# Cross-attention and routed experts: scores of batch 1 in their own banks, and the mask loaded for VectorE from batch 3 on

## The reference

```python
# x (16, 100, 128), ctx (16, 1444, 128), mask (16, 1444) with 1 at keys left out
def xattn(input, memory, mask, w_input, dot_scale):
    input_dot = einsum('bqd,od->bqo', input, w_input)
    cross_dot = einsum('bqd,bkd->bqk', input * dot_scale, memory)
    att = input_dot + cross_dot - 1e+30 * mask[:, None, :]
    return einsum('bqk,bkd->bqd', softmax(att), memory)

def ffn(x):                         # 8 experts of width 512, the best 2 of each row
    gates, indices = top_k(softmax(einsum('bsd,ed->bse', x, W_router)), 2)
    gates = gates / sum(gates)
    return sum over the experts e of weight_e * (silu(x Wg_e) * (x Wu_e)) Wd_e

x = x + tanh(g_xattn) * xattn(layernorm(x), ctx, mask, w_input, dot_scale)
x = x + tanh(g_ffn) * ffn(layernorm(x))
```

## Time and profile before

| | |
|---|---|
| median of three runs | 260.19 us (258.18 to 261.61) |
| the profiled execution | 261.3 us, its span 259.5 us |
| TensorE busy | 231.3 us, 89% of the span |
| VectorE, ScalarE, GpSimd busy | 138.6, 115.1 and 114.0 us |
| chain that ended last | PE 73%, DMA 6%, issue 6%, DVE 6%, POOL 4% |
| attention steps | to about 136 us of the span |
| experts | to about 242 us |
| gather and add | the rest |

### The profile page before, as it was taken

How to read it: one execution, slowest core, us unless ns; L and a number is a source line. 1 busy time by engine, 2 the same in 40 slices (tenths; PEclk the granted TensorE clock), 3 DMA queues, 4 the chain that set the end, 5 groups by cost and what they waited for, 6 DMA issues and landing times.

```text
span 259.5 us, 5485 instructions
## 1 busy us (share of the span) xinstructions
PE 231.3 (89%) x1448; PEld 181.9 (70%) x1449; DVE 138.6 (53%) x499; ACT 115.1 (44%) x269; POOL 114.0 (44%) x197
## 2 busy tenths in 40 slices
PE   7979999999999999979998899799999999999200
PEld 6437877677777677847868688688888789888100
DVE  4237565766868768685686567333433333432043
ACT  3024553446554445623646435355554455545000
POOL 4451433365675566544456764443352333224300
PEclk9979999999999999997999999999999999999755
DMA  6997677788786776835923521232111111000194
GB/s 171 330 380 222 191 258 207 244 282 246 235 320 201 260 268 198 305 114 145 377 71 86 196 77 34 63 82 63 45 51 53 41 43 39 30 23 21 37 240 132
DMA packets 19107, 41.39 MB, mean 159 GB/s; under 512 B 3574, under 2 KB 10018, under 8 KB 19070
## 3 DMA queue, kind: packets, MB, share of 16 engines
q1 hardware_dynamic: 15796, 36.37, 44.0%
q0 software_dynamic: 2560, 3.77, 4.6%
q10 hardware_dynamic: 726, 0.94, 1.4%
HBM read 34.82 MB, written 6.24 MB: 158 GB/s over the span
## 4 chain that ended last, share of the span: by engine, by line
PE 73%; DMA 6%; issue 6%; DVE 6%; POOL 4%; ACT 1%; SPq 1%; ACTq 1%; DVEq 0%; POOLq 0%
PE psum L1084 16%; PE psum L1064 12%; PE psum L1178 10%; PE psum L1156 6%; PE psum L1158 5%; PE psum L1157 5%; PE psum L1073 5%; PE psum L1167 4%; PE psum L1052 4%; DMA ctx_sb<-results 3%; PE psum L1146 1%; POOL slots L553 1%; DMA w_lo<-in_mask 1%; PE psum L1092 1%; DMA slots<-pair_rows,slot_i 1%
## 5 line engine op out<-in xcount | busy, mean ns | idle before, releaser
L1084 PE MATMUL psum<-ctx_sb,probsT 128*100 128x128 f32 (+1 forms) x384 | 53.9, 286 | 0.0
L610 POOL DMA_INDIRECT results<-y_sb,dest x32 | 30.7, 959 | 52.4 <-DVE dest L968 24.9
L1084 PEld LDWEIGHTS psum<-ctx_sb,probsT 128*100 128x100 f32 (+1 forms) x384 | 45.0, 170 | 3.4 <-issue 0.7
L979 DVE SCALAR_TENSOR_TENSOR scores<-probs,row_in,psum 128x512 f32<-128x512 f32 x32 | 23.9, 747 | 38.4 <-ACT probs L696 38.2
L1064 PE MATMUL psum<-ctxT,qT 128*100 128x512 f32 (+1 forms) x96 | 44.1, 597 | 0.0
L635 ACT ACTIVATE probsT<-psum 128x400 f32<-128x400 f32 x48 | 20.7, 504 | 52.2 <-PE psum L1073 52.1
L553 POOL DMA_INDIRECT slots<-pair_rows,slot_i x32 | 33.9, 1061 | 18.6 <-DMA slots<-pair_rows,slot_i 9.4
L786 DVE CUSTOM_DVE_ANT_0 scores<-psum,zeros 100x1444 f32<-100x1444 f32 x16 | 26.6, 1661 | 18.7 <-PE psum L1064 18.7
L1178 PE MATMUL psum<-w_down,hidT 128*128 x256 | 34.3, 277 | 1.9 <-issue 0.7
L696 ACT ACTIVATE probs<-psum 128x512 f32<-128x512 f32 x32 | 19.2, 599 | 35.3 <-PE psum L1158 35.3
L1178 PEld LDWEIGHTS psum<-w_down,hidT 128*128 128x128 f32 x256 | 31.1, 192 | 2.6 <-issue 2.6
(11 more groups left out here) (134 smaller groups left out, 306.6 us busy)
## 6 DMA issues: line engine op xcount, KB each, us to landing
ctxT<-in_ctx_cols SPq DMA_DIRECT2D x16, 722.0 KB, 4.7
ctx_sb<-in_ctx SPq DMA_DIRECT2D x16, 704.0 KB
w_raw<-in_w_experts SPq DMA_DIRECT2D x16, 256.0 KB, 3.4
row_in<-slots SPq DMA_DIRECT2D x32, 65.0 KB, 1.9
w_down<-in_w_experts SPq DMA_DIRECT2D x4, 512.0 KB, 7.2
slots<-empty SPq DMA_DIRECT2D x8, 195.0 KB, 2.2
ctx_sb<-results SPq DMA_DIRECT2D x4, 192.0 KB, 5.1
ctx_sb<-results ACTq DMA_DIRECT2D x4, 192.0 KB, 5.9
```

Of the source, the lines that this page charges most:

```text
L610: nc.gpsimd.indirect_dma_start(results, bass.IndirectOffsetOnAxis(ap=dest[:, s:s + 1], axis=0), y_sb[:, s, :], None).then_inc(y_stored[s], 16)
L979: nc.vector.scalar_tensor_tensor(out=hidden[k % 2], in0=silu[k % 2], scalar=row_in[:, o, D:D + 1], in1=up_ps[k % 2], op0=ALU.mult, op1=ALU ...
L1084: last = nc.tensor.matmul(attn_ps[0:Q, 0:D], probsT[0:rows[c], c, :], ctx_sb[0:rows[c], b % CTX_RING, c, :], start=(c == 0), stop=(c == CH ...
```

## The change

Six things change.

1. The scores of batch 1 go to banks 3 to 5 (`second_scores_ps`), so they no longer wait for VectorE's reduce of batch 0. These are the banks of the transposes; the first transposes of probabilities wait for `scores_done` of batch 1, with eight matmuls of no use ahead of them, and scores of batch 1 wait until ScalarE has copied q out of bank 3.
2. For batch 0 the scores come first and the mask is added behind them. Its columns are loaded ahead of the mask.
3. The mask is added by TensorE for batches 0 to 2 alone (`PE_MASKS` = 3). ScalarE scales the mask by -1e30 once more into a tile, stores it to a tensor in memory (`mask_scaled`), and from batch 3 on SP loads one row of it into 100 partitions of `maskb` (two transfers, 96 and 4 partitions, three batches ahead). VectorE's reduce adds `maskb` where it added `zeros`, and waits for its load.
4. The tables are spread: `tile_counts` stays in step 12, `tile_runs` goes to step 13, `tile_rows` stays in 14, `tile_experts` goes to 15, and the gates go ahead of the tables of their step.
5. In step 15 GpSimd makes the rows of batch 13 first and scatters those of batch 10 then.
6. In the experts, the transpose of tile 8's rows comes behind down of tile 5 on TensorE and ScalarE alike, the expert's number is read earlier for three tiles, and down of tile 30 writes to a bank of its own (`other_y_ps`), so that down of tile 31 need not wait for its copy.

The order on VectorE in step 12 and at the head of step 13, before: the last of `top_two`, `tile_counts` and `tile_runs`, then the gates, then the residual (L763).

```diff
--- before.py
+++ after.py
@@ -28,6 +28,8 @@
+MASK_RING = 3
+PE_MASKS = 3
...
@@ -115,10 +119,12 @@
+        other_y_ps = psum[:, 6, 0:D]
...
-        zeros = sb("zeros", [Q, K])
+        maskb = sb("maskb", [Q, MASK_RING, K])
+        zeros = maskb[:, (PE_MASKS + MASK_RING - 1) % MASK_RING, :]
...
@@ -336,6 +346,14 @@
+        def scores_home(b):
+            return second_scores_ps if b == 1 else scores_ps
+        def y_home(k):
+            return other_y_ps if k == T - 2 else y_ps
         def pairs(j, m):
...
@@ -366,6 +384,11 @@
+            def load_mask(b):
+                s = b % MASK_RING
+                sp.dma_start(maskb[0:MAIN, s, :], mask_scaled[b, 0:K].partition_broadcast(MAIN)).then_inc(mask_in[s], 16)
+                sp.dma_start(maskb[MAIN:Q, s, :], mask_scaled[b, 0:K].partition_broadcast(Q - MAIN)).then_inc(mask_in[s], 16)
             def load_weights(b):
...
@@ -376,10 +399,10 @@
             load_x(0)
+            load_cols(0)
             sp.dma_start(mask_raw[0:B * PIECES, :], pieces).then_inc(mask_loaded, 16)
...
             sp.dma_start(mask_raw[LOW:mask_rows, :], pieces).then_inc(mask_loaded, 16)
-            load_cols(0)
...
@@ -390,12 +413,16 @@
             load_x(3)
+            sp.wait_ge(scaled_stored, 16)
+            load_mask(PE_MASKS)
...
                 sp.wait_ge(scores_done, b + 1)
+                if b + MASK_RING < B:
+                    load_mask(b + MASK_RING)
                 for c in ROUNDED.get(b + 1, ()):
...
@@ -570,13 +597,12 @@
             for b in range(B):
-                if b == B - 1:
-                    pair_landed(0)
-                    scatter(b - 5)
                 if b >= 2:
...
                     normalise2(b - 2)
-                if 5 <= b < B - 1:
+                if b == B - 1:
+                    pair_landed(0)
+                if 5 <= b:
                     scatter(b - 5)
...
@@ -675,6 +701,9 @@
             copy_qT(0)
+            nc.scalar.activation(mask_f32, mask_raw[0:B * PIECES, :], ACT.Copy, scale=NEG).then_inc(scaled_done, 1)
+            act.wait_ge(scaled_done, 1)
+            act.dma_start(mask_scaled.rearrange("b (t n) -> (b t) n", n=PIECE), mask_f32).then_inc(scaled_stored, 16)
             for b in range(B):
...
@@ -700,14 +729,14 @@
                     nc.scalar.activation(hidT[:, (k - 1) % 2, :], hidT_ps, ACT.Copy).then_inc(hidT_done, 1)
-                if k == EARLY - 1:
-                    rowT_high(i, k + 1)
                 if k - 2 >= 0:
...
                     wait(act, y_stored[s], i * 16 + 16 * ((k - 2) // YRING))
-                    nc.scalar.activation(y_sb[:, s, :], y_ps, ACT.Copy).then_inc(y_done, 1)
+                    nc.scalar.activation(y_sb[:, s, :], y_home(k - 2), ACT.Copy).then_inc(y_done, 1)
+                if k == EARLY - 1:
+                    rowT_high(i, k + 1)
...
@@ -783,7 +812,10 @@
                 apart(dve)
-                nc.vector.tensor_tensor_reduce(out=scores[0:Q, :], in0=scores_ps[0:Q, 0:K], in1=zeros[:, :],
+                if b >= PE_MASKS:
+                    dve.wait_ge(mask_in[b % MASK_RING], 32 * ((b - PE_MASKS) // MASK_RING + 1))
+                addend = maskb[:, b % MASK_RING, :] if b >= PE_MASKS else zeros
+                nc.vector.tensor_tensor_reduce(out=scores[0:Q, :], in0=scores_home(b)[0:Q, 0:K], in1=addend,
                                                scale=1.0, scalar=LOWEST, op0=ALU.add, op1=ALU.max,
...
@@ -1032,40 +1066,54 @@
-            def keep_warm(n):
+            def keep_warm(n, into=ring_ps[GROUPS - 1][:, (GROUP - 1) * Q:GROUP * Q]):
                 for _ in range(n):
-                    nc.tensor.matmul(ring_ps[GROUPS - 1][:, (GROUP - 1) * Q:GROUP * Q], identity[:, :], identity[:, 0:Q], start=True, stop=True)
+                    nc.tensor.matmul(into, identity[:, :], identity[:, 0:Q], start=True, stop=True)
...
-            def add_mask(b):
+            def add_mask(b, start):
                 pe.wait_ge(select_done, 1)
                 pe.wait_ge(mask_lo_done, 1)
-                wait(pe, scores_done, b)
-                wait(pe, rank_done, (b - 3) // 2)
                 for t, n in enumerate(range(0, K, PIECE)):
                     m = min(PIECE, K - n)
-                    nc.tensor.matmul(scores_ps[0:Q, n:n + m], select[:, b * PIECES + t:b * PIECES + t + 1].to_broadcast([mask_rows, Q]), mask_split[:, 0:m], start=True, stop=False)
-            def score(b):
-                if b > 0:
-                    add_mask(b)
+                    last = nc.tensor.matmul(scores_home(b)[0:Q, n:n + m],
+                                            select[:, b * PIECES + t:b * PIECES + t + 1].to_broadcast([mask_rows, Q]),
+                                            mask_split[:, 0:m], start=start, stop=not start)
+                return last
+            def add_scores(b, start, stop):
                 pe.wait_ge(qT_done, b + 1)
                 pe.wait_ge(col_loaded[b % COL_RING], 16 * (b // COL_RING + 1))
-                wait(pe, scores_done, b)
-                wait(pe, rank_done, (b - 3) // 2)
                 for n in range(0, K, 512):
                     m = min(512, K - n)
-                    last = nc.tensor.matmul(scores_ps[0:Q, n:n + m], qT[:, b % 2, :], ctxT[:, b % COL_RING, n:n + m],
-                                            start=False, stop=True)
-                last.then_inc(scores_raw, 1)
+                    last = nc.tensor.matmul(scores_home(b)[0:Q, n:n + m], qT[:, b % 2, :], ctxT[:, b % COL_RING, n:n + m],
+                                            start=start, stop=stop)
+                return last
+            def score(b):
+                if b == 0:
+                    add_scores(0, True, False)
+                    add_mask(0, False).then_inc(scores_raw, 1)
+                    return
+                if b == 1:
+                    pe.wait_ge(qT_done, 2)
+                else:
+                    pe.wait_ge(scores_done, b)
+                    wait(pe, rank_done, (b - 3) // 2)
+                if b < PE_MASKS:
+                    add_mask(b, True)
+                add_scores(b, b >= PE_MASKS, True).then_inc(scores_raw, 1)
             def transpose_probs(b):
+                if b == 0:
+                    keep_warm(8, attn_ps[:, 0:Q])
+                    pe.wait_ge(scores_done, 2)
                 pe.wait_ge(probs_done, b + 1)
...
@@ -1130,10 +1178,9 @@
-            keep_warm(10)
-            add_mask(0)
+            keep_warm(11)
             transpose_q(0)
-            keep_warm(2)
+            keep_warm(1)
             for b in range(B):
...
@@ -1167,15 +1218,20 @@
-            def down(i, k):
+            def down(i, k, e=None):
                 n = i * YRING + k
                 o = k % 2
-                e = pe.value_load(tile_expert[0:1, bass.ds(n, 1)], min_val=0, max_val=E - 1)
+                e = expert_of(i, k) if e is None else e
                 pe.wait_ge(hidT_done, n + 1)
-                wait(pe, y_done, n)
+                if k == T - 2:
+                    pe.wait_ge(rank_done, LAST + 1)
+                elif k == T - 1:
+                    pe.wait_ge(y_done, T - 2)
+                else:
+                    wait(pe, y_done, n)
                 for c in range(FC):
-                    last = nc.tensor.matmul(y_ps, hidT[:, o, c * P:(c + 1) * P], w_down[:, bass.ds(e * F + c * P, P)],
+                    last = nc.tensor.matmul(y_home(k), hidT[:, o, c * P:(c + 1) * P], w_down[:, bass.ds(e * F + c * P, P)],
                                             start=(c == 0), stop=(c == FC - 1))
...
@@ -1204,16 +1259,19 @@
                 if k - 2 >= 0:
-                    down(i, k - 2)
+                    down(i, k - 2, e)
+                if k == EARLY - 1:
+                    transpose_rows(i, k + 1)
...
             transpose_xn2(B - 3)
+            pe.wait_ge(experts_ready, 1)
+            first = expert_of(0, 0)
             transpose_probs(B - 1)
             route(B - 3)
-            pe.wait_ge(experts_ready, 1)
             pe.wait_ge(w_lo_done, B)
-            gate_up(0, 0)
+            gate_up(0, 0, first)
             ranks(LAST - 1)
...
```

More of the change, by code:

```diff
@@ L94, in build @@
     slots = nc.dram_tensor("slots", [DUMMY + P, ROW], F32).ap()
+    mask_scaled = nc.dram_tensor("mask_scaled", [B, mask.shape[1]], F32).ap()
     results = nc.dram_tensor("results", [2 * TOKENS + YRING * P, D], F32).ap()
@@ L234, in build @@
         mask_lo_done = sem("mask_lo_done")
+        scaled_done = sem("scaled_done")
+        scaled_stored = sem("scaled_stored")
+        mask_in = [sem(f"mask_in{s}") for s in range(MASK_RING)]
         ctx_loaded = [sem(f"ctx_loaded{s}") for s in range(CTX_RING)]
@@ L928, in step @@
                     tile_rows(False)
+                if b == 15:
                     tile_experts(False)
[L930 to L931 removed]
                 for c in split[1:]:
                     split_weights(c)
[L935 removed]
+            nc.vector.memset(zeros, 0.0)
             dve.wait_ge(identity_done, 1)
```

21 lines of the change are left out of this document (12 added, 9 removed).

## The result

The changed kernel took 277.02 us (median of four runs, 276.31 to 278.06), the kernel before 259.68 beside it. The ratio is 1.067 (95% interval 1.059 to 1.075): slower, 23 us above the forecast. The profiled execution took 276.75 us, its span 275.0.

The account below looks back on a forecast made before the run. TensorE's own order was taken to bound the kernel (73% of the span). 0.4 + 1.6 + 1.6 + 2.97 - 1.06 + 0.1 + 0.4 + 0.4 + 0.2 = 6.6 us off 260.2 gave 253.6 us, range 249.5 to 259.5.

Parts of the forecast that it names:

- The prediction's rival: Attention's DMA queue becomes the bound because of the mask loads: 257.6 us (chance 10%) or 265.7 us (chance 8%).
- 10 us as slack: DMA queue in attention: loads ordered two to three steps early were counted as 10 us it could owe without loss.
- the bad case: DMA queue in attention: each mask load takes 3.8 us, giving 265.7 us in all, chance 8%.
- The start: Batches 0 and 1: scores 0 start at 8.0 us (7.7 to 9.0), gaining 0.4 us.
- Masks on TensorE: Steps 3 to 15 without mask matmuls: gain 1.6 us in 3 and 4, 1.6 in even 6 to 12, odd 0.
- the chain from the residual: Attention steps: VectorE's residual through GpSimd's pair_rows to TensorE's transpose of xn2 takes 3.33 us, so odd steps gain 0.
- Tables: Table operations moved out of step 12: step 13 gains 2.97 us, 1.50 of it the clock; step 14 loses 1.06.
- the 1.50 that I had charged for this: Step 14: TensorE idles 1.89 us, so its clock falls there and costs 1.50 us.
- Step 15: Rows made ahead of scatters on GpSimd: gain 0.1 us, with the last exp as the next limit.
- Experts: Expert tiles: gains of 0.4 us at tile 8, 0.4 at the last down, 0.2 from expert numbers loaded earlier.
- the longer wait that the prediction had named for late scatters: Tile 8 of the experts: would wait longer if GpSimd's queue came late; costed at nothing.
- The two terms of the last tiles: End of the experts: 0.4 us from the last down not awaiting ScalarE's copy, 0.2 from expert numbers loaded earlier.

## Why the prediction was wrong

**DMA: the step that failed.** The prediction's rival had the right mechanism: the queue becomes the bound, and it "would show on ScalarE first, waiting for w_raw". Its price was wrong, in the sentence "at the 363 GB/s that a full stretch showed (share 1.01) 1.6 us. Then 5.94 + 1.6 = 7.54, as long as the new step". It took the best eleven microseconds for the rate of a full queue. Full stretches of the changed kernel moved 262 to 295 GB/s; the 2.51 MB of a step take 9.5 us at 265 GB/s, and the step took 9.48. The 5.94 us were share times length at a queue that was a quarter idle; the same 1.93 MB need 7.3 at 265. The other term of the same sum, "of which I count 10 us as slack", had no row behind it, and it failed too. Ten steps took 94.79 us from batch 5 to 15, and 77.95 without masks: 16.8 were lost. At 265 GB/s ten such steps owe 10 x (9.5 - 7.80) = 17, so from batch 5 on no slack shows. ScalarE waits for weights in step 5 already. One row read a hundred times, the reason that the rival gave for a high price, was not it. With 8% and 265.7 us the bad case was both too rare and too short, though its sign, ScalarE waiting for w_raw with no wait for maskb, came as written. The Trainium skill, page "DMA: Bandwidth & Descriptors", section "Measured (HBM→SBUF, 128 partitions, SWDGE, issued from GpSimd)", gives 341 GB/s for 1 MB and 138 for 64 KB; transfers of 256 to 722 KB moved 262 to 323 in full windows here, between the two. That the size of the transfers is the reason is not shown: with masks of half the size, loaded twice, the windows moved more, 287 to 323.

**The start: the second step that failed.** Predicted a gain of 0.4 with "I take 8.0 us" for scores 0, at worst 9.0; they started at 10.85, and batch 2 came 2.91 us late, and some 5 us late against the other executions with the old start. The copy of q was named as standing behind the rounding, but what it costs the mask to stand behind 722 KB of columns was not priced.

**Masks on TensorE: right.** Counted as the prediction counts, from S to S (without masks S is the start of the scores), the kernel without masks gave 1.28 us in steps 3 and 4 (15.44 before, 14.16), forecast 1.6; in steps 6, 8, 10 and 12 0.39, 0.63, 0.46 and 0.64, together 2.12, forecast 1.6 between 0.8 and 2.3; in steps 5, 7, 9 and 11 no more than 0.02 each, forecast 0. In step 9 without masks the transpose of xn2 came 4.31 us after the scores' start, forecast 4.3; in step 10 3.77, forecast 3.6 to 4.0; steps 3 and 4 in the changed kernel 3.53 and 3.54, forecast about 3.4. That the chain from the residual holds the odd steps is shown twice, by the kernel without masks and by the one with odd masks loaded. TensorE's waits for pair_rows came to 5.9 us there and 6.0 in the changed kernel, forecast near 8.

**Tables: the steps right, the clock's share not.** Step 13 (S to S) took 2.68 us less without masks (10.91 before, 8.23), forecast 2.97; step 14 took 0.94 more, forecast 1.06. The new wait in step 14 was 1.55 us there, forecast 1.89, and the clock did not fall behind it; the 1.50 that I had charged for this was not due. But of the 2.97, 1.50 was the clock, taken from one execution of the kernel before, and the same wait of 1.73 us in the kernel with the tables back left the clock up. So this part is not the tables' to give. In the profiles of the two kernels with TensorE's masks the spread tables give only 0.14 us from batch 12 to 15 (25.20 and 25.06, scores to scores); the rest of what they are worth shows in step 15, where the kernel with the tables back waits 1.00 us for VectorE's rowT_lo and 1.21 for its `choose`. The prediction had nothing there. The experiment on the tables alone gives 1.8 us; the prediction's terms without the mask are 2.97 - 0.83 - 1.06 = 1.08.

**Step 15: wrong.** Forecast 0.1. With TensorE's masks the stretch from batch 15 to the end of the table took 13.32 us against 14.16: 0.84 won. Without masks it took 17.92. The prediction named the exp as the next limit; the rows of tile 0 come before it. Up to its transpose (136.85 before) step 15 did give 0.42 us without masks; the 3.41 behind it, at the low clock, were not in the sum. The rows wait for scatters, and came 2.5 us sooner when the 2 MB of w_down were sent behind them.

**Experts: too good.** Tile 8 was to give 0.4. From the end of the table to its gate matmul it is 24.03 us both before (143.37 to 167.40) and with TensorE's masks (144.47 to 168.50): 0. The work that was put in front filled no gap; the wait, 0.57 in the earlier trace rows, became 1.39, the longer wait that the prediction had named for late scatters and put at nothing. The two terms of the last tiles, 0.6 together, show as 0.2 (74.52 less 74.32 us from there to the end of the last down).

**The sum with what was measured.** Without masks: start -3.28, batches 2 to 15 +5.94, step 15 -3.76, which leaves -1.1; the median says -1.5. The loads take 15.6 more.

## What to carry to other kernels

A queue whose busy share is 0.76 is not one quarter free: divide the step's new bytes by the step's length and ask whether a full queue of this kernel ever moved that much for longer than a few microseconds, since the best stretch is no rate to plan with (2.51 MB in 7.53 us are 333 GB/s, and no window of 13 us or more moved over 323). What comes late is not the transfer that was added but whatever has the least lead behind it in the same queue, and the engine that waits for it holds up work that has nothing to do with it. Before giving up a good exchange of one engine's work for bytes, halve the bytes: in bf16, and with the small load of the start kept ahead of the big one, this change is worth 2%, against 0.4% for the same version with TensorE's masks.

## What the runs showed of the hardware

A full set of queues moved 262 to 323 GB/s over windows of 13 to 15 us in attention, against 363 from 8.5 to 19.5 us before the change; 7.5 MB more cost 40 us of transfer time, 3.8 MB only 13. Reading one row of memory into a hundred partitions cost no more than reading a hundred rows (277.0 and 279.0 us). TensorE's granted clock fell to 1.2 GHz behind idle times of 3.93 us (step 7) and of 1.15 and 0.59 us close together (step 15 without masks, where the same matmuls then took 1.5 to 1.9 times as long), and did not fall behind a single one of 1.55 us (step 14 there: 3.68 us from the transpose to the next S, 3.72 before). Behind one of 1.73 us it fell in the kernel before and stayed up in the one with the tables back, so the length of one wait alone does not settle it. Executions of one start differ too: the scores of batch 1 took 3.88 us before and 2.59 with the same start in the kernel with TensorE's masks and the old start.
